# The last rounding pass of the FFN's weights: adding DMAs issued by GpSimd in place of a VectorE subtraction

## The chip, the cores and the metric

One core of a Trainium2 chip. The metric is the device time of one execution in microseconds, as the median over several runs. The engines are called by the profile's names: PE (TensorE), DVE (VectorE), ACT (ScalarE), POOL (GpSimd) and SP (SyncE, which here only issues DMAs).

## The reference

x is 2048 tokens by 512 features. The first layer normalizes x, projects it to q, k and v (16 heads of 32), and runs a chunked test-time-training scan: for each chunk of 16 tokens the state S of every head is read (k S and q S), a gradient-like v_new is made from it, and S is updated before the next chunk may read it. A gate, a norm and Wo follow, and the result is normalized and added to x. The second layer is a gated FFN (512 to 1536 to 512) with weights rounded to float8_e4m3:

```
wq = w.astype(jnp.float8_e4m3fn).astype(x.dtype)
gate = silu((x @ gate_wq) * gate_scale);  up = (x @ up_wq) * up_scale
y = ((gate * up) @ down_wq) * down_scale
```

So before the FFN can multiply, each of its 3 x 512 x 1536 weights has to be rounded to the values that float8_e4m3 has. The kernel does that itself, in float32 arithmetic.

## The kernel before

The 2048 tokens are 16 tiles of 128, and a tile is 8 chunks; "chunk 2.5" is chunk 5 of tile 2. All engines run the same timeline `body(t, s, h)` over the tiles, each its own list of instructions in a written order, tied by semaphores. In the body of tile t the scan of tile t runs; beside it the projections of tile t + 1 ("prep"), the tail of the attention of tile t - 1 ("post"), and the FFN of pairs of earlier tiles, cut into six rounds.

One chunk goes so. PE reads the state (`read_state`, L558 and L567). DVE's `scan_front` opens with a statistic (L1465) on it. POOL makes rho from that, a power of -1/2 (`scan_rho`, L1180), then rho2 and re. DVE's `scan_back` needs rho at L1487 and ends with VX (L1501). PE's `write_state` (L581, L589) multiplies VX, and DVE adds the product to the state (`scan_state`, SQ at L1508). PE may then read it for the next chunk. Work of the other stages is placed between these steps: on DVE between VX and the state sum, or behind the state sum and in front of the next L1465; on PE between the state read and the update, or behind the update. POOL's own roots of 16 columns (rk in chunk 3, rq in chunk 1, ro in chunk 5; 16 of each) are powers at L1180 too.

The rounding works on 36 units of 128 x 512 weights, one per chunk from chunk 0.0 to chunk 4.6 (none for chunk 2 of tiles 1 to 3; `unit_at`). A unit u takes these steps, all but the loads one chunk's length apart at most:
- SP loads it into buffer `wst[u % 2]`, which is a `yb` tile (`stage`, L357). The load of unit u + 2 waits until unit u is rounded (L396).
- DVE extracts a power of two from each weight's exponent into `wmg`, which is `x1[3]` (`exponent`, L1609), at the end of the chunk.
- ACT makes the "magic" number from it in two passes (`magic`, L998 and L1000), in the next chunk.
- `shift` subtracts: wst = wmg - wst. POOL does it behind VX (L1268) where `pool_free` holds; in chunk 3, and in chunks 1 and 5 from tile 1 on, DVE does (L1614): 26 and 10 units.
- DVE subtracts again and writes the weight matrix GW, UW or DW: w = wmg - wst (`quantize`, L1619).

The FFN's first products wait for their thirds of the weights (L637, L657). DVE's list of one chunk ends with shift (if it is DVE's), quantize and the exponent of the next unit; then comes the next chunk's `scan_front`.

PE's clock falls when it is little used. The prologue keeps it up with products that nobody reads (`idle`, L430: each call makes 2n products of 128 x 256, which are 4n PE instructions).

## Time and profile before

| | |
|---|---|
| median of 3 runs | 890.64 us (889.45 to 890.83) |
| the profiled execution | 887.37 us |
| its span (first to last instruction) | 885.6 us |
| PE busy | 793.8 us, 90% |
| DVE busy | 676.8 us, 76% |
| ACT busy | 496.7 us, 56% |
| POOL busy | 480.5 us, 54% |
| granted PE clock, mean | 0.953 |

A busy share is an average over the whole span. Which engine sets the pace differs between the stretch with the rounding (the first 284 us) and the rest, so the views by stretch and the waits matter more than this table. All times of the trace count from the span's start.

### The profile page before, as it was taken

The page shows a single profiled execution, that of the slowest core. Times are in us where ns is not written, and L with a number is a line of the kernel's source. Part 1 is how long each engine was busy: PE and PEld are TensorE (multiplying, and loading weights), DVE is VectorE, ACT ScalarE, POOL GpSimd, SP SyncE. Part 2 cuts the span into 40 slices and gives each one's busy share as a digit, 9 for nine tenths or more (in the row PEclk, how much of TensorE's full clock was granted, in tenths as well). Part 3 has the DMA queues.
Part 4 walks back from the last instruction along what each step waited for, and adds up shares of the span by engine and source line. Part 5 has one row for each costly group of instructions (what it writes and reads, how often), then busy time and mean ns, then how long its engine had stood idle before and what let it go on. Part 6 is the DMA issues. An engine that isn't in the chain of part 4 may idle for free.

```text
span 885.6 us, 22947 instructions
## 1 busy us (share of the span) xinstructions
PE 793.8 (90%) x8308; PEld 558.6 (63%) x8308; DVE 676.8 (76%) x2704; ACT 496.7 (56%) x1328; POOL 480.5 (54%) x848
## 2 busy tenths in 40 slices
PE   9867777688978999999999999999999999978896
PEld 4444444456566666667676676766676766766795
DVE  3688887788878787778787878778777878767444
ACT  2776675667657565655646475656565564633331
POOL 6355756565556656556465546565665646445300
PEclk9887798798989999999999999999999999979998
DMA  8012121211211001000100010000100010001000
GB/s 274 25 49 61 34 64 36 62 37 37 61 37 37 2 2 49 2 26 2 49 2 26 1 38 14 26 1 2 50 2 25 3 48 2 2 2 48 1 24 25
DMA packets 16721, 28.48 MB, mean 32 GB/s; under 512 B 3520, under 2 KB 3520, under 8 KB 16608
## 3 DMA queue, kind: packets, MB, share of 16 engines
q1 hardware_dynamic: 16608, 27.02, 9.9%
q8 instruction: 66, 1.08, 0.5%
q14 instruction: 47, 0.39, 0.1%
HBM read 22.82 MB, written 4.19 MB: 31 GB/s over the span
## 4 chain that ended last, share of the span: by engine, by line
PE 59%; DVE 17%; POOL 10%; ACT 7%; issue 6%; DMA 1%; SPq 1%; POOLq 0%; DVEq 0%; ACTq 0%
PE bank L630 17%; PE bank L426 15%; PE bank L663 8%; PE bank L606 4%; PE bank L581 4%; POOL rho L1180 3%; PE bank L440 3%; PE bank L558 2%; ACT BDk L893 2%; PE bank L567 2%; PE bank L589 2%; DVE work L1492 2%; DVE f L1574 1%; PE bank L454 1%; DVE work L1496 1%
## 5 line engine op out<-in xcount | busy, mean ns | idle before, releaser
L1180 POOL TENSOR_TENSOR rho<-sy,cst 128x2 f32<-128x2 f32 x128 | 89.5, 700 | 236.4 <-DVE sy L1465 236.4
L581 PEld LDWEIGHTS bank<-VX,BDkR 128*64 128x64 f32 x1024 | 45.1, 140 | 93.1 <-issue 53.1
L1508 DVE TENSOR_TENSOR SQ<-SQ,bank 128x128 f32<-128x128 f32 x128 | 36.6, 286 | 79.2 <-PE bank L581 78.0
L581 PE MATMUL bank<-VX,BDkR 128*64 128x64 f32 x1024 | 57.0, 233 | 40.4 <-DVE VX L1501 40.4
L948 ACT ACTIVATE qhR<-bank 128x64 f32<-128x64 f32 x128 | 28.2, 221 | 102.6 <-PE bank L589 102.0
L907 ACT ACTIVATE BDkR<-kR,cst 128x128 f32<-128x128 f32 x256 | 81.3, 397 | 0.0
L663 PE MATMUL bank<-DW,fh 128*128 128x512 f32 x188 | 80.4, 428 | 0.6 <-DVE fl L1581 0.6
L893 ACT ACTIVATE BDk<-bank 32x256 f32<-32x256 f32 x124 | 46.4, 374 | 53.8 <-DVE kR L1407 46.1
L663 PE MATMUL bank<-DW,fl 128*128 128x512 f32 x188 | 75.2, 400 | 0.0
L1487 DVE SCALAR_TENSOR_TENSOR work<-work,rho,rR 128x32 f32<-128x32 f32 x256 | 53.1, 248 | 25.9 <-POOL rho L1180 25.7
L558 PEld LDWEIGHTS bank<-SQ,BDk 128*64 128x64 f32 x1024 | 46.2, 142 | 38.5 <-issue 34.4
L567 PE MATMUL bank<-SQ,BDq 128*64 128x32 f32 x1024 | 54.8, 228 | 16.2 <-ACT qhR L948 15.0
L630 PE MATMUL bank<-xh,UW 128*128 128x256 f32 x384 | 66.2, 295 | 1.2 <-DVE f L1574 1.2
L630 PE MATMUL bank<-xh,GW 128*128 128x256 f32 x384 | 65.9, 294 | 1.4 <-DVE xl L1563 1.3
L558 PE MATMUL bank<-SQ,BDk 128*64 128x48 f32 x1024 | 57.2, 233 | 9.7 <-DVE SQ L1508 8.2
L426 PE MATMUL bank<-Wq,xnT 128*64 128x512 f32 x256 | 63.3, 633 | 0.7 <-ACT xnT L840 0.7
L606 PE MATMUL bank<-Wo,o 128*64 128x512 f32 x256 | 61.1, 621 | 1.7 <-DVE o L1545 1.7
L426 PE MATMUL bank<-Wv,xnT 128*64 128x512 f32 x256 | 62.5, 607 | 0.0
L630 PE MATMUL bank<-xl,GW 128*128 128x256 f32 x384 | 62.3, 285 | 0.0
L630 PE MATMUL bank<-xl,UW 128*128 128x256 f32 x384 | 61.6, 283 | 0.0
L426 PE MATMUL bank<-Wk,xnT 128*64 128x512 f32 x256 | 60.3, 611 | 0.0
L567 PEld LDWEIGHTS bank<-SQ,BDq 128*64 128x64 f32 x1024 | 44.8, 146 | 19.6 <-ACT qhR L948 11.6
(168 smaller groups left out, 2149.4 us busy)
## 6 DMA issues: line engine op xcount, KB each, us to landing
xt<-in_x SPq DMA_DIRECT2D x16, 256.0 KB, 2.8
x<-in_x SPq DMA_DIRECT2D x16, 256.0 KB, 2.8
out<-x SPq DMA_DIRECT2D x16, 256.0 KB, 2.1
yb<-in_gate_w SPq DMA_DIRECT2D x12, 256.0 KB, 2.7
yb<-in_up_w SPq DMA_DIRECT2D x12, 256.0 KB, 2.7
yb<-in_down_w SPq DMA_DIRECT2D x12, 256.0 KB, 2.7
Wk<-in_wk SPq DMA_DIRECT2D x1, 1024.0 KB, 6.1
Wv<-in_wv SPq DMA_DIRECT2D x1, 1024.0 KB, 7.9
```

Of the source, the lines that this page charges most:

```text
L426: ins = mm(dst[lo, :], half(xnT, k, lo), W[:, k * n:(k + 1) * n], start=(k == 0), stop=(k == KD - 1), skip_group_check=True)
L558: ins = mm(KAv[gp * 64:(gp + 1) * 64, gh, 0:48], bdk(s)[:, gh * NC + j, gp, :], SQv[:, 2 * gh + gp, :], start=True, stop=True, skip_group_ ...
L567: ins = mm(QH[gp * 64:(gp + 1) * 64, gh * DH:(gh + 1) * DH], bdq[:, j // 4, 2 * gp + gh, j % 4, :], S[:, 2 * gh + gp, :], start=(gh == 0), ...
L581: ins = mm(dS[p, e], bdkr[:, gh, j % 4, p], VX[:, e], start=True, stop=True, skip_group_check=True)
L606: ins = mm(PA[1][lo, :], half(ogT, g, lo), Wo[:, g * D:(g + 1) * D], start=(g == 0), stop=(g == 3), skip_group_check=True)
L630: ins = mm(b[:, q * PAIR:(q + 1) * PAIR], W[:, k * I + m * P:k * I + (m + 1) * P], part[:, k * PAIR:(k + 1) * PAIR], start=(part is xh and ...
L663: ins = mm(Y[k][:, :], part[:, q * PAIR + k * P:q * PAIR + (k + 1) * P], DW[:, m * D:(m + 1) * D], start=(m == 0 and n == 0), stop=(m == M ...
L893: ins = fn(bdk(s)[q, :, gp, own(h)], PA[1][p:p + 32, 256 * a:256 * a + 256].rearrange("p (m c) -> p m c", c=CH), ACT.Copy)
L907: ins = fn(bdkr[:, :, place, h * DH:(h + 1) * DH], kR[:, :].rearrange("p (gh j e) -> p gh j e", gh=2, e=DH)[:, :, js], ACT.Identity, scale ...
L1180: tt(dst, src, cst[:, C_NH:C_NH + n], ALU.pow).then_inc(*one)
L1487: stt(out=g2(g)[:, gh], in0=g2(u)[:, gh], scalar=rho[:, gh:gh + 1], in1=r_j[:, gh, :], op0=ALU.mult, op1=ALU.add).then_inc(*scan_v.one(f"g ...
L1508: tt(S, S, dS.rearrange("p (g e) -> p g e", e=DH), ALU.add).then_inc(*scan_v.one("S"))
```

## The change

The last subtraction goes from DVE to a DMA. ACT's second pass now writes the magic number straight into the unit's place in GW, UW or DW. POOL makes wst = wst - place for all 36 units, and then issues a DMA from wst onto the place that adds: place + (w - place). DVE keeps only the exponent. The semaphore for a rounded unit becomes two, one per buffer, counted in 16s, and those who wait for rounded weights wait for both. DVE's next exponent may start when ACT has read `wmg` (it waits for `s_magic`). In the chunks where `pool_free` doesn't hold, shift and DMA stand at the end of POOL's list of the chunk, behind its root. SP's load of unit u + 2 waits for the landing of unit u's adding DMA.

Two smaller parts come with it, both on PE. The gate product of tiles 2 and 3 moves from chunk 0 of its tile to chunk 6 of the tile before, behind the centring product. And unread products (`idle`) are put between state read and update: in tile 0 in chunks 4, 6 and 7 (12, 12 and 8 PE instructions), in tiles 1 and 2 in chunk 4 (12 each).

```diff
-        def quantized(third, n):
-            return s_quant, 12 * third + n
+        def quantized(n, k):
+            return s_quant[k], 16 * ((n + 1 - k) // 2)
+
+        def place(u):
+            w, e = unit(u)
+            return (GW, UW, DW)[w][:, e:e + D]
...
-                        sp.wait_ge(s_quant, UNITS)
+                        sp.wait_ge(s_magic, UNITS)
...
-                            sp.wait_ge(s_quant, u + 1)
+                            sp.wait_ge(s_quant[u % 2], 16 * (u // 2 + 1))
                             stage(u + 2)
...
             def prep_gate(t):
                 if early(t):
                     pe.wait_ge(*prep_a.at("g1", t))
+                    if t > 1:
+                        pe.wait_ge(*prep_a.at("th", t - 1))
...
             def ffn_g(p, r):
                 if p == 0:
-                    pe.wait_ge(*quantized(r // 2, 8))
+                    pe.wait_ge(*quantized(12 * (r // 2) + 8, 0))
+                    pe.wait_ge(*quantized(12 * (r // 2) + 8, 1))
...
-                        if early(t) and t > 1:
-                            prep_gate(t)
...
                     if j == 4 and early(t + 1):
                         prep_v_early(t + 1, (3,))
+                        pe.wait_ge(*(prep_v.at("kR", t) if t else prep_v.at("rR", 0)))
+                        idle(3, cst)
...
                         if early(t + 1):
                             prep_cen(t + 1)
+                            if t == 0:
+                                pe.wait_ge(*prep_v.at("kR", 1))
+                                idle(3, cst)
+                            else:
+                                prep_gate(t + 1)
...
                     if j == 7 and t == 0:
                         prep_gate(1)
+                        idle(2, cst)
...
-                fn(wmg[:, :], wmg[:, :], ACT.Identity, bias=epses[:, 6:7]).then_inc(s_magic, 1)
+                fn(place(u), wmg[:, :], ACT.Identity, bias=epses[:, 6:7]).then_inc(s_magic, 1)
...
             def shift(u):
                 pool.wait_ge(s_magic, u + 1)
-                tt(wst[u % 2][:, :], wmg[:, :], wst[u % 2][:, :], ALU.subtract).then_inc(s_shift, 1)
+                tt(wst[u % 2][:, :], wst[u % 2][:, :], place(u).bitcast(F32), ALU.subtract).then_inc(s_shift, 1)
+
+            def quantize(u):
+
+                pool.wait_ge(s_shift, u + 1)
+                nc.gpsimd.dma_start(place(u).bitcast(F32), wst[u % 2][:, :], accum_op=ALU.add).then_inc(s_quant[u % 2], 16)
...
                             shift(u)
+                            quantize(u)
...
+                    if scan and not pool_free(t, j):
+                        for u in unit_before(t, j):
+                            after_rows(NC * t + j)
+                            shift(u)
+                            quantize(u)
...
                 if u:
-                    dve.wait_ge(s_quant, u)
+                    dve.wait_ge(s_magic, u)
...
-            def shift(u):
-                dve.wait_ge(s_magic, u + 1)
-                tt(wst[u % 2][:, :], wmg[:, :], wst[u % 2][:, :], ALU.subtract).then_inc(s_shift, 1)
-
-            def quantize(u):
-                w, e = unit(u)
-                dve.wait_ge(s_shift, u + 1)
-                tt((GW, UW, DW)[w][:, e:e + D], wmg[:, :], wst[u % 2][:, :], ALU.subtract).then_inc(s_quant, 1)
...
-                    for u in unit_before(t, j):
-                        if not pool_free(t, j):
-                            shift(u)
-                        quantize(u)
```

## Rows read from the trace of the kernel before

**Rows 1.** Busy time by stretch, cut at tiles' starts: stretch and its length, PE, PEld, DVE, ACT, POOL busy, PE clock.

```profile
26.70:73.50 46.80, 33.12 (x392) 21.46 (x392) 36.09 (x152) 33.09 (x87) 23.38 (x39) 0.84 0.15 41
73.50:121.60 48.10, 37.49 (x396) 21.42 (x396) 40.02 (x159) 31.77 (x81) 28.49 (x42) 0.80 0.16 45
...
172.80:225.30 52.50, 44.03 (x466) 30.41 (x467) 43.26 (x169) 35.73 (x90) 31.70 (x51) 0.87 0.16 47
225.30:284.20 58.90, 50.02 (x514) 35.37 (x514) 47.25 (x178) 38.25 (x94) 33.58 (x52) 0.94 0.16 46
284.20:332.50 48.30, 46.68 (x518) 32.97 (x517) 39.64 (x165) 29.10 (x81) 28.84 (x55) 1.00 0.03 7
```

**Rows 2.** Line L1465 from 32 to 284 us: its instructions; idle time before them, times.

```profile
L1465 DVE BATCH_NORM_STATS2 sy<-bank x39: 221/228/236, 32.2 to 277.5; 128x6 f32<-128x68 f32 x39
...
  PE bank L558: 1.4, 1
```

**Rows 3.** Timeline of DVE, chunk 2.5: start, us, line, operation, count, [idle before it].

```profile
154.02 0.41 DVE L1487 SCALAR_TENSOR_TENSOR work<-work,rho,rR 128x32 f32<-128x32 f32 x2 [0.18 <-POOL rho L1180]
...
155.99 0.29 DVE L1508 TENSOR_TENSOR SQ<-SQ,bank 128x128 f32<-128x128 f32 x1
...
157.02 0.66 DVE L1614 TENSOR_TENSOR yb<-x,yb 128x512 f32<-128x512 f32 x1
157.72 0.69 DVE L1619 TENSOR_TENSOR UW<-x,yb 128x512 fp32r<-128x512 f32 x1
158.51 0.43 DVE L1609 TENSOR_SCALAR x<-yb 128x512 int32<-128x512 int32 x1
158.86 0.23 DVE L1465 BATCH_NORM_STATS2 sy<-bank 128x6 f32<-128x68 f32 x1
```

**Rows 4.** Timeline of PE, chunk 2.5: its read of the state.

```profile
156.43 0.44 PE L558 MATMUL bank<-SQ,BDk 128*64 128x48 f32 x8 [0.27 <-DVE SQ L1508]
```

**Rows 5.** Groups of instructions, whole span: count, busy us, mean ns, idle before.

```profile
L1268 POOL TENSOR_TENSOR yb<-x,yb 128x512 f32<-128x512 f32 x26 | 35.1, 1350 | 33.3 <-DVE VX L1501 23.8 <-ACT x L1000 9.5
...
L1619 DVE TENSOR_TENSOR DW<-x,yb 128x512 fp32r<-128x512 f32 x12 | 9.3, 771 | 0.4 <-POOL yb L1268 0.2
...
L1619 DVE TENSOR_TENSOR GW<-x,yb 128x512 fp32r<-128x512 f32 x12 | 9.1, 760 | 0.1
...
L1619 DVE TENSOR_TENSOR UW<-x,yb 128x512 fp32r<-128x512 f32 x12 | 8.4, 704 | 0.1
...
L1614 DVE TENSOR_TENSOR yb<-x,yb 128x512 f32<-128x512 f32 x10 | 6.7, 665 | 0.0
```

**Rows 6.** Timeline of POOL, chunk 2.5: its root of 16 columns.

```profile
154.58 2.90 POOL L1180 TENSOR_TENSOR ro<-oss,cst 128x16 f32<-128x16 f32 x1
```

**Rows 7.** Timeline of DVE, chunk 1.3.

```profile
93.83 0.41 DVE L1487 SCALAR_TENSOR_TENSOR work<-work,rho,rR 128x32 f32<-128x32 f32 x2 [0.99 <-POOL rho L1180]
```

**Rows 8.** Timeline of SP: one issue of a load of 256 KB.

```profile
29.79 0.33 SPq L385 DMA_DIRECT2D xt<-in_x  x1
```

**Rows 9.** DMA issues: count, KB each, median us from issue to landing.

```profile
out<-x SPq DMA_DIRECT2D x16, 256.0 KB, 2.1
yb<-in_gate_w SPq DMA_DIRECT2D x12, 256.0 KB, 2.7
```

**Rows 10.** Busy time by stretch, as rows 1, of chunk 1.0.

```profile
73.50:80.00 6.50, 5.71 (x44) 2.57 (x44) 4.21 (x20) 3.90 (x9) 2.34 (x4) 0.58 0.25 81
```

**Rows 11.** Timeline of DVE, chunk 1.0: its state sum.

```profile
78.66 0.29 DVE L1508 TENSOR_TENSOR SQ<-SQ,bank 128x128 f32<-128x128 f32 x1 [1.12 <-PE bank L581]
```

**Rows 12.** Timeline of PE: prologue, chunk 0.6 and chunk 1.0.

```profile
7.91 1.08 PE L434 MATMUL bank<-work 128*64 128x256 f32 x8
...
64.57 0.45 PE L581 MATMUL bank<-VX,BDkR 128*64 128x64 f32 x8 [2.07 <-DVE VX L1501]
...
74.50 3.68 PE L426 MATMUL bank<-Wq,xnT 128*64 128x512 f32 x8 [0.69 <-ACT xnT L840]
```

**Rows 13.** Waits from 20 to 284 us: who for whom, us in all, times, longest.

```profile
DVE work L1487 <- POOL rho L1180: 8.8, 40, 1.0
```

More of the change, by code:

```diff
@@ L181, in build @@
         s_stage = [sem(f"s_stage{n}") for n in range(len(wst))]
-        s_exp, s_over, s_magic, s_shift, s_quant = (sem(n) for n in ("s_exp", "s_over", "s_magic", "s_shift", "s_quant"))
+        s_exp, s_over, s_magic, s_shift = (sem(n) for n in ("s_exp", "s_over", "s_magic", "s_shift"))
+        s_quant = [sem(f"s_quant{n}") for n in range(2)]
         s_mask = sem("s_mask")
@@ L656, in ffn_down @@
                     if p == 0:
-                        pe.wait_ge(*quantized(r // 2, 12))
+                        pe.wait_ge(*quantized(12 * (r // 2) + 12, 0))
+                        pe.wait_ge(*quantized(12 * (r // 2) + 12, 1))
                     if r == 0 and p > 0:
@@ L1587, in fin_y @@
                 else:
-                    dve.wait_ge(s_quant, UNITS)
+                    dve.wait_ge(*quantized(UNITS, k))
                 if p == 0 and k == 0:
```

## The prediction

> **What bounds the kernel now.** I read the windows cut at the starts of tiles 0 to 5 first. Tile 5, the first with no weights to round, takes 48.3 us, and the PE is busy for 46.7 of it at full clock. Tiles 0 to 3 take 46.8 to 52.5 us, but their PE is busy for only 33 to 44 us and its granted clock is 0.80 to 0.87 (tile 4 is 58.9 us at 0.94) [rows 1]. So up to about 284 us something other than the PE sets the pace, and all the rounding lies there. Next the line that opens each chunk, the VectorE's L1465: in chunks 0.1 to 4.7 (tile.chunk, 39 of them) it waited for the PE once, for 1.4 us in all [rows 2]. It is otherwise behind other VectorE work.
>
> The timeline of chunk 2.5 shows which. The VectorE has written VX by 155.44, the PE answers with the update, and the state sum SQ runs from 155.99 to 156.28. Then come a statistic of the next x, the shift (0.66), the rounding subtraction L1619 (0.69) and the exponent (0.43), until the next chunk opens at 158.86 [rows 3]. The PE's read of the state started at 156.43 and ended at 156.87 [rows 4]: the answer lay there 2 us before it was read. From SQ's end the PE needs 0.59 us in such a chunk. The rest is what a lighter VectorE can win, until the PE's answer or another resource is late.
>
> **What the change takes off the VectorE.** 36 subtractions L1619 are 9.3 + 9.1 + 8.4 us and 10 shifts L1614 are 6.7 us: 33.5 us, all of it in front of an L1465 that doesn't wait for the PE [rows 5]. The state sum of these chunks is not delayed by it. Where the PE has products of its own in front of the state read, the gain stops at its end: chunk for chunk that costs 1.6 us of the 33.5.
>
> **What it puts on POOL.** The 26 shifts that POOL has stay (1.35 us of its time each, 1.27 undisturbed), the 10 others come to it, and 36 DMAs are issued there [rows 5]. POOL also computes rho, on which the VectorE waits in every chunk, so anything that is still running on POOL 0.31 us after a chunk opens delays the chunk. There are two sorts of chunk.
> - Where POOL has a root of 16 columns (2.90 us, chunk 2.5 as the example: from 154.58 to 157.48 [rows 6]; chunks 1 and 5 of a tile, and 3), the shift and DMA go behind it. The old next opening was 158.86; less shift and subtraction it would be 157.5. POOL would end at 157.48 + 1.27 + 0.1 + the issue. With an issue of 1.0 us that is 159.85, and rho, wanted at 157.8, is 2 us late where 1.35 was won. Ten units are of this sort.
> - Elsewhere the shift starts just after VX, is done 3.9 us after the opening, and with the DMA POOL is free at 5.0: in time where nothing follows (chunks 0, 5, 7), late by up to 3 us where POOL's own list goes on. In chunk 1.2 it goes on so far that rho of 1.3 was late by 0.8 us already (L1487 waited 0.99 us for it, against the usual 0.18 [rows 3, 7]). The issue is added to that whole, and the VectorE gets there 1.75 us sooner: 3.4 us late.
>
> **The issue is not in the trace.** From below: SP spends 0.33 us on issuing 256 KB [rows 8]. From above: a POOL instruction over a whole tile, 1.35 us [rows 5], and somewhat beyond, since an adding DMA has two tiles to address: 1.5 us. Nothing makes it a gain. I take 1.0 us, nearest to the POOL rows since POOL does the work, and 0.3 and 1.5 for the range.
>
> **The landing isn't either.** Plain DMAs of 256 KB land 2.1 us (store) and 2.7 us (load of weights) after their issue [rows 9]. The adding one reads twice. I take 2.6 us after POOL has issued, from 2.1 to 4. It matters since SP loads unit u+2 into the buffer of unit u only after the landing, and the VectorE's exponent of u+2, which stands in order in front of the next chunk's opening, waits for that load. The loop of one buffer is: exponent 0.43, opening to VX 2.55, shift until 3.9, wait and issue until 5.0, landing 7.6, load 10.4, exponent. It may take two chunks, 10.6 to 12 us. So it just fits in the light chunks, and is 1 to 2 us late behind a chunk with a root. What queues behind the waiting exponent is the whole chain: the next chunk's statistics, rho, VX, the state.
>
> **The sum.** I carried these rules through chunks 0.0 to 5.7 in order, with each chunk's own VectorE work, PE times and POOL list; on the old placement they give the start of tile 6 within 0.3 us of the trace's. For the change: 33.5 us off, 1.6 back at the PE's end, 22.6 back where rho is later, 10.4 back in exponents that wait for their load, and 5.1 off again, since in chunks where the PE was late anyway (it ends its own products after VX) a late VX costs less. Together -4.0 us. The two unseen prices decide: 0.3 and 2.1 give -16.0; 1.0 and 2.1 give -5.9; 1.3 and 2.6 give +2.1; 1.5 and 3.0 give +9.8; 1.0 and 4.0 give +7.8.
>
> **The gate and the unread products.** The gate of tiles 2 and 3 moves from chunk 0 to chunk 6 of the tile before. In chunk 0 it ran in front of the VectorE's VX; in chunk 6 it runs there too, behind a centring that in chunk 0.6 left the PE idle for the last 2.07 us before the update [rows 12]: 16 PE instructions of 128 columns, about 1.1 us at full clock, fit. Nothing, either way, with 0.5 us each at half clock if they don't. The products are 56 PE instructions at 0.135 us (1.08 us for 8 [rows 12]), 7.6 us in all, at most 12 at a time (1.6 us) between the state read and the update, where the PE idled about 2 us [rows 12]: nothing at full clock, though 3.2 us each at half clock, which would hold the update by up to 1 us in five chunks. What they can bring is clock. Chunk 1.0 ran at 0.58 [rows 10]: 8 instructions on Wq took 3.68 us [rows 12], which at full clock would be half, and the state sum waited 1.12 us for the update behind them [rows 11]. If they hold, that wait goes, plus 0.1 to 0.2 us in some ten chunks whose update ran slow. I take -1.5 us, from -3 to +4. SP's x loads, and the FFN's waits for units 8, 20, 32 and 12, 24, 36, come over a microsecond after the landings: nothing.
>
> **Two rules of the Trainium skill.** The shift and exponent rows show a VectorE instruction with one input over 512 elements at 0.43 us where one with two takes 0.66 or more [rows 3, 5]. The Trainium skill's page "SBUF — State Buffer", section "SBUF: two separate sides", says that a GpSimd-issued DMA's descriptors can't be written while the VectorE runs in its two-port mode; the exponent falls about where POOL would issue. No run here shows it. By that rule half of the issues would take 0.43 us more, and my sum would lose some 4 us: it would be about zero. The page "DMA: Bandwidth & Descriptors", section "Anatomy of one DMA — SWDGE (gpsimd) path", puts a whole DMA of this kind at 2.0 us plus bytes / 436 GB/s, an estimate of 2.6 us for 256 KB where I took 3.6 for issue and landing, though it is a figure for plain copies; by it the sum would be 3 us better.
>
> **The rivals.**
> - POOL is cheap: the issue costs what SP's does, the landing is a store's. -16 - 2: 872.6 us. For it: SP's row. Against: POOL's rows are two to four times those of the VectorE for the same tile.
> - The loop of load, rounding, adding and loading is too long (slower). It decides from the point where issue and landing together pass 3.2 us in light chunks: each exponent then waits, up to 29 us in the sum at 1.0 and 4.0, and the time is 890.6 + 7.8 = 898.4 us; with a dear issue (1.5, 3.0) rho carries it instead: 900.4. For it: the load must follow the landing, and ten units are late already. Against: nothing in the trace takes 4 us for 256 KB with the queues empty.
> - The relief and POOL's lateness cancel (1.2 and 2.6, or the lock above): within 1.8 us of 890.6.
>
> **How the numbers follow.** The profiled execution was 887.4 us, 1.8 around a span of 885.6; the median is 890.64, and I take the difference off that: -4.0 - 1.5 = -5.5, 885.1 us. Chances: forecast (876 to 888.8) 0.38, cheap POOL (below 876) 0.19, cancel 0.13, slower rival 0.30. Within 0.2% (1.8 us, about what can be told from no change) is 0.13. The range from 873 to 900 leaves out the ends.
>
> **What would show it.** Right: tiles 0 to 4 together shorter by 4 to 7 us, tiles from 5 on unchanged; L1487 waiting for rho over 1 us in chunks 2, 4, 6 and those behind a root, some 20 us over the 8.8 of now [rows 13]; about 10 us of waits in front of L1609 for loads. Wrong: rho waits as now (issue below 0.3), or L1609 waiting in nearly every chunk (landing near 4), or L581 behind unread products.

## The result and the profile after

The changed kernel takes 907.53 us (median of 4 runs, 905.43 to 908.25) against 890.1 us before (4 runs, 889.45 to 890.83). The ratio is 1.0194, with a 95% interval of 1.018 to 1.0208: slower by 17.4 us. The forecast was 885.1 us, faster by 5.5, in a range from 873 to 900. Size and sign were wrong. The profiled execution of the changed kernel took 905.43 us, its span is 903.6 us and its mean granted clock 0.952.

The lines of the kernel have moved: L1465 is now L1493, L1487 L1515, L1475 L1503, L1609 L1637, L1268 L1285, L1508 L1536, L1400 L1428, and the new DMA is L1290. L1268 is now POOL's product qR over a whole tile (L1251 before).

First the windows cut at the starts of tiles 0 to 5, as [rows 1] (stretch and length; PE, PEld, DVE, ACT, POOL busy; clock; DMA). Tile 2 of before, which [rows 1] leaves out, then all of after:

```profile
121.60:172.80 51.20, 36.55 (x404) 20.80 (x400) 42.21 (x169) 32.12 (x81) 31.00 (x50) 0.87 0.16 48
```

```profile
30.30:78.70 48.40, 36.69 (x422) 23.70 (x423) 33.02 (x144) 33.24 (x87) 31.30 (x47) 0.83 0.33 72
78.70:128.60 49.90, 35.97 (x412) 21.32 (x410) 37.23 (x151) 31.20 (x80) 37.54 (x51) 0.89 0.37 80
128.60:184.00 55.40, 38.71 (x411) 21.95 (x408) 38.63 (x160) 32.52 (x82) 40.24 (x60) 0.85 0.35 77
184.00:241.50 57.50, 44.02 (x459) 29.84 (x459) 39.69 (x161) 35.99 (x90) 40.94 (x60) 0.82 0.33 74
241.50:301.10 59.60, 50.65 (x523) 35.75 (x521) 40.73 (x167) 38.06 (x94) 44.86 (x63) 0.94 0.35 77
301.10:350.60 49.50, 47.63 (x522) 33.69 (x521) 39.71 (x166) 29.02 (x81) 28.77 (x55) 1.00 0.07 17
```

Tiles 0 to 4 are longer by 1.6, 1.8, 4.2, 5.0 and 0.7 us, 13.3 in all, tile 5 by 1.2. The DVE's busy time in tiles 0 to 4 fell by 3.1, 2.8, 3.6, 3.6 and 6.5 us, 19.5 together, where 33.5 us of instructions were taken off it. POOL's rose by 8 to 11 us a tile. The first chunk also opens later, at 30.3 instead of 26.7 us. Most of that is scatter between executions: it opens at 27.3 to 28.6 us in the three experiments without GpSimd's DMAs and at 27.0 to 31.0 in the nine with them, and SP's issue of Wg in front of it took 1.67 us in the trace of before, 4.23 here, and from 1.67 to 4.29 in the traces of the experiments, with and without those DMAs. That a microsecond of it belongs to the change is not excluded. So single traces are compared by their tiles below, not by their spans.

The second view is the page's chain that ended last, by engine; of before, then of after.

```profile
PE 59%; DVE 17%; POOL 10%; ACT 7%; issue 6%; DMA 1%; SPq 1%; POOLq 0%; DVEq 0%; ACTq 0%
```

```profile
PE 52%; POOL 18%; DVE 12%; issue 6%; ACT 5%; DMA 5%; SPq 0%; POOLq 0%; ACTq 0%; DVEq 0%
```

The DVE's share of the path fell by 5 points, as meant. POOL's rose by 8 and the DMAs' by 4. The groups say at which prices (line, engine, operation, count, busy us, mean ns, idle before). First a row of before that is not among those ahead of the prediction, then after:

```profile
L1475 DVE SCALAR_TENSOR_TENSOR work<-mP,work 128x64 f32<-128x64 f32 x128 | 27.5, 215 | 0.0
```

```profile
L1503 DVE SCALAR_TENSOR_TENSOR work<-mP,work 128x64 f32<-128x64 f32 x128 | 33.2, 259 | 0.0
L1637 DVE TENSOR_SCALAR x<-yb 128x512 int32<-128x512 int32 x36 | 22.2, 617 | 6.5 <-DMA yb<-in_gate_w 3.2 <-DMA yb<-in_down_w 2.3 <-DMA yb<-in_up_w 1.0
...
L1290 POOL DMA_DIRECT2D GW<-yb x12 | 11.2, 932 | 3.6 <-POOL yb L1285 3.6
L1290 POOL DMA_DIRECT2D UW<-yb x12 | 11.1, 922 | 3.6 <-POOL yb L1285 3.6
L1290 POOL DMA_DIRECT2D DW<-yb x12 | 11.0, 916 | 3.6 <-POOL yb L1285 3.6
```

And from the DMA issues, as [rows 9] (KB, median us from issue to landing):

```profile
UW<-yb POOLq DMA_DIRECT2D x12, 256.0 KB, 3.4
```

An issue costs POOL 0.92 us and 0.30 us of idle time between the end of the shift and the DMA (3.6 us for 12), 1.22 us together, 36 times: 44.1 us. The landing comes 3.4 us after the start of the issue, 2.4 to 2.5 after its end. And two instructions of the DVE have become longer without having changed: the exponent from 0.425 us [before, 15.3 us for 36] to 0.617, and L1503 from 0.215 to 0.259: 6.9 and 5.7 us.

The third view is the DVE's waits in tiles 0 to 4 (who for whom: us in all, times, longest). Before, beside the row for rho in [rows 13]:

```profile
DVE SQ L1508 <- PE bank L581: 17.3, 18, 2.9
...
DVE kss L1391 <- ACT xn_dv_rT L871: 4.9, 2, 2.6
DVE bx L1400 <- POOL bt L1208: 3.8, 4, 1.9
```

After:

```profile
DVE work L1515 <- POOL rho L1197: 26.1, 39, 2.0
DVE SQ L1536 <- PE bank L590: 15.9, 15, 2.9
DVE bx L1428 <- POOL bt L1225: 9.2, 5, 2.9
DVE kss L1419 <- ACT xn_dv_rT L888: 7.7, 2, 4.6
...
DVE x L1582 <- ACT x L981: 3.5, 1, 3.5
DVE x L1637 <- DMA yb<-in_gate_w: 3.2, 4, 1.3
DVE x L1637 <- DMA yb<-in_down_w: 2.3, 3, 1.5
...
DVE x L1637 <- DMA yb<-in_up_w: 1.0, 2, 0.8
```

The wait for rho is 17.3 us longer. The other names belong to the preparation of the next tile (bt, kss) and to the tail of an earlier one (nb_f, x). bt, another output of POOL, is waited for by 5.4 us more, and kss by 2.8, over ACT, which in its turn waited for POOL's nb_f for 13.2 us in these tiles instead of 8.2 (7.36 us of it in chunk 2.2, where the DVE then waited 4.64 us for kss). The loads take 6.5.

One place shows how the new list of POOL works on both engines. In chunk 2.4 POOL goes from the shift to the DMA to qR; then the DVE's exponent of the same chunk (start, us, line, operation, [idle before]):

```profile
160.57 1.27 POOL L1285 TENSOR_TENSOR yb<-yb,UW 128x512 f32<-128x512 f32 x1 [1.19 <-DVE VX L1529]
162.14 0.94 POOL L1290 DMA_DIRECT2D UW<-yb  x1 [0.30 <-POOL yb L1285]
162.80 1.59 POOL L1268 TENSOR_TENSOR qR<-qR,bR 128x512 f32<-128x512 f32 x1
```

```profile
162.65 2.02 DVE L1637 TENSOR_SCALAR x<-yb 128x512 int32<-128x512 int32 x1
```

The exponent starts at 162.65, while POOL issues, and ends at 164.67, 0.28 us after qR did, for 0.43 us of work. It is not the issue alone that does this. In chunk 0.2 an exponent lies wholly inside an issue, with no whole-tile POOL instruction beside it, and keeps its length (POOL, then DVE):

```profile
47.01 0.91 POOL L1290 DMA_DIRECT2D GW<-yb  x1 [0.31 <-POOL yb L1285]
```

```profile
47.21 0.42 DVE L1637 TENSOR_SCALAR x<-yb 128x512 int32<-128x512 int32 x1
```

Of the 36 exponents 8 took over 0.5 us, and 7 of these ran beside a whole-tile POOL instruction, a shift or qR; with an issue alone beside them six took 0.41 to 0.43 us and one 0.57. What makes the three of 2.0 to 2.5 us is the pair: they start during an issue, before qR's record starts, and end 0.3 us behind qR. L1503 is the same: its 8 instances over 0.5 us all overlap a shift or POOL's whole-tile product L1275, and the longest, 1.79 us in chunk 1.3, starts in an issue.

And behind the root of chunk 2.5, the case that the prediction took as its example, in chunk 2.6:

```profile
169.16 1.43 POOL L1285 TENSOR_TENSOR yb<-yb,UW 128x512 f32<-128x512 f32 x1
170.90 0.94 POOL L1290 DMA_DIRECT2D UW<-yb  x1 [0.30 <-POOL yb L1285]
171.56 1.03 POOL L1197 TENSOR_TENSOR rho<-sy,cst 128x2 f32<-128x2 f32 x1
```

```profile
172.69 0.41 DVE L1515 SCALAR_TENSOR_TENSOR work<-work,rho,rR 128x32 f32<-128x32 f32 x2 [2.01 <-POOL rho L1197]
...
177.33 0.36 DVE L1428 TENSOR_TENSOR bx<-bt,cst 128x64 f32<-128x64 f32 x2 [1.69 <-POOL bt L1225]
```

The DVE waits 2.01 us for rho, of which 0.18 is usual: some 1.8 us late, where 2 was worked out. The same lateness then runs on in POOL's list: VX is late, the next shift and DMA with it, bt stands behind that DMA, and the DVE waits another 1.69 us in the same chunk. That second wait was not in the sum.

### The profile page after: what moved, and what is told of

Its sections match the earlier page's. It is cut to its first block, busy times and chain, and to the rows that moved or that the text cites. A ratio compares the mean times of both kernels' runs of the same rounds, so it can differ in the third digit from the quotient of the medians.

```text
span 903.6 us, 23071 instructions
## 1 busy us (share of the span) xinstructions
PE 799.1 (88%) x8364; PEld 561.8 (62%) x8364; DVE 657.5 (73%) x2658; ACT 496.9 (55%) x1328; POOL 527.4 (58%) x894
## 4 chain that ended last, share of the span: by engine, by line
PE 52%; POOL 18%; DVE 12%; issue 6%; ACT 5%; DMA 5%; SPq 0%; POOLq 0%; ACTq 0%; DVEq 0%
PE bank L639 16%; PE bank L433 14%; PE bank L674 7%; POOL rho L1197 4%; POOL yb L1285 4%; PE bank L590 3%; PE bank L615 3%; PE bank L447 3%; PE bank L567 2%; POOL rq L1197 2%; PE bank L576 2%; POOL ro L1197 2%; ACT BDk L910 2%; DVE work L1520 1%; PE bank L598 1%
## 5 line engine op out<-in xcount | busy, mean ns | idle before, releaser
L1197 POOL TENSOR_TENSOR rho<-sy,cst 128x2 f32<-128x2 f32 x128 | 93.4, 730 | 194.1 <-DVE sy L1493 193.9
L1536 DVE TENSOR_TENSOR SQ<-SQ,bank 128x128 f32<-128x128 f32 x128 | 36.6, 286 | 77.7 <-PE bank L590 76.5
L1515 DVE SCALAR_TENSOR_TENSOR work<-work,rho,rR 128x32 f32<-128x32 f32 x256 | 53.1, 248 | 43.8 <-POOL rho L1197 43.1
```

The lines of the kernel that those rows point to most:

```text
L1197: tt(dst, src, cst[:, C_NH:C_NH + n], ALU.pow).then_inc(*one)
L1515: stt(out=g2(g)[:, gh], in0=g2(u)[:, gh], scalar=rho[:, gh:gh + 1], in1=r_j[:, gh, :], op0=ALU.mult, op1=ALU.add).then_inc(*scan_v.one(f"g ...
L1536: tt(S, S, dS.rearrange("p (g e) -> p g e", e=DH), ALU.add).then_inc(*scan_v.one("S"))
```

## The experiments

Three theories were to be told apart. Theory 1: POOL's time for the issues, which delays rho and what stands behind it in POOL's list. Theory 2: the DVE's instructions are slowed while POOL issues. Theory 3: the loop of load, add and next load is too long. All runs are compared with the kernel before on the same chip (medians 889.8 to 890.0 us).

**The two halves of the change.** `small_alone` is the kernel before with this alone:

```diff
 def prep_gate(t):
                     pe.wait_ge(*prep_a.at("g1", t))
+                    if t > 1:
+                        pe.wait_ge(*prep_a.at("th", t - 1))
...
-                        if early(t) and t > 1:
-                            prep_gate(t)
...
+                        pe.wait_ge(*(prep_v.at("kR", t) if t else prep_v.at("rR", 0)))
+                        idle(3, cst)
...
+                            if t == 0:
+                                pe.wait_ge(*prep_v.at("kR", 1))
+                                idle(3, cst)
+                            else:
+                                prep_gate(t + 1)
...
+                        idle(2, cst)
```

> The kernel before with the gate of tiles 2 and 3 behind the centring and with the unread products; the rounding stays as it was. Theory (the whole loss is the adding DMAs'): my -1.5 us stands, within -3 to +1 of the kernel before, 887 to 891 us, and the prologue ends where it did, first chunk at 26.7 us. Rival (the unread products and the gate hold up the update): 3 to 4 us slower, with the state sum L1508 waiting for L581 more than before in tiles 0 to 2.

889.27 us, ratio 0.9991 (0.9977 to 1.0006). `dma_alone` is the changed kernel with these lines taken back:

> The changed kernel with the gate where it was and without the unread products. Theory (the loss is the adding DMAs'): the ratio of the changed kernel within 3 us, 906 to 911 us. Rival (the small parts are what costs): under 895.

909.16 us, ratio 1.0215 (1.0188 to 1.0242). So the loss is the rounding's alone, and the small parts bring 1 to 2 us or nothing. They do not do what I took them for: in chunk 1.0 of `small_alone` the update still came late behind products on Wq at the lower clock (timelines of PE and DVE). In the changed kernel these 8 instructions took 1.94 us instead of 3.68, but in `dma_alone`, without the unread products, they took 1.94 as well:

```profile
76.15 3.68 PE L426 MATMUL bank<-Wq,xnT 128*64 128x512 f32 x8 [0.69 <-ACT xnT L848]
```

```profile
80.31 0.29 DVE L1516 TENSOR_TENSOR SQ<-SQ,bank 128x128 f32<-128x128 f32 x1 [1.12 <-PE bank L583]
```

**The relief without its price.** `no_adds` is the changed kernel with the DMA taken out. A unit counts as done when POOL has shifted it; the last addition of the rounding is thus left out.

```diff
-                tt(wst[u % 2][:, :], wst[u % 2][:, :], place(u).bitcast(F32), ALU.subtract).then_inc(s_shift, 1)
+                tt(wst[u % 2][:, :], wst[u % 2][:, :], place(u).bitcast(F32), ALU.subtract).then_inc(s_quant[u % 2], 1)
...
-                nc.gpsimd.dma_start(place(u).bitcast(F32), wst[u % 2][:, :], accum_op=ALU.add).then_inc(s_quant[u % 2], 16)
+                pass
```

> The changed kernel with its 36 adding DMAs left out (so the weights stay the magic numbers, not the rounded weights); all 36 shifts stay on POOL and a buffer is free as soon as the shift is done. Theory that the loss is what the issuing of the DMA costs (POOL's time, some 1.2 us each with the gap, and the VectorE instructions that run longer beside it) and its landing: all of the 33.5 us off the VectorE shows except what the PE and the 10 late shifts give back, some 865 to 875 us; the exponent is back at about 0.43 us mean. Rival that the 10 shifts behind the roots are the cost: 885 to 895. If POOL's shift and not its DMA makes the exponent long, the mean of the exponent stays near 0.6 us.

872.46 us, ratio 0.9804 (0.979 to 0.9819): 17.6 us faster than before. The exponent is short again, and the wait for rho is up from 9 to 17 us, where POOL's list has only the shifts behind the roots more than before (group, and wait over 27 to 290 us):

```profile
L1636 DVE TENSOR_SCALAR x<-yb 128x512 int32<-128x512 int32 x36 | 15.7, 436 | 0.0
```

```profile
DVE work L1514 <- POOL rho L1197: 17.4, 43, 1.9
```

The adding DMAs therefore cost 907.5 - 872.5 = 35.1 us, twice what the rest of the change brings.

**The DMA put on top of the kernel before.** `issue_only` leaves the rounding as it was and issues 35 adding DMAs in vain:

```diff
+            def add_nothing(u):
+                if u == 0:
+                    pool.wait_ge(s_wq, 16)
+                    pool.wait_ge(s_void, 1)
+                else:
+                    pool.wait_ge(s_add, 16 * u)
+                if u < UNITS - 1:
+                    nc.gpsimd.dma_start(DW[:, 11 * D:12 * D].bitcast(F32), Wq[:, 0:D], accum_op=ALU.add).then_inc(s_add, 16)
```

> The kernel before (subtractions and all on the VectorE as they were) with 35 adding DMAs of 256 KB issued by POOL at the places of the change, onto a place that is not yet written, and for which only the last subtraction waits. Theory 1 (POOL's time for the issue delays rho and its other outputs): +10 to +20 us, waits of L1487 for rho up from 9 to some 20 us. Theory 2 (the VectorE's instructions run longer beside the issue): mean of the exponent and of the two-input instructions up by the same 0.1 to 0.2 us as in the changed kernel, some 10 us of the loss. Theory 3 (the loop of load, add and load costs): under 2 us, since nobody waits for the landing. Prologue: if a GpSimd DMA in the program is what delays Wk's landing and the first chunk (26.7 to 30.3 us), it does here too; if not, 26.7.

903.23 us, ratio 1.0147 (1.0128 to 1.0167): 13.2 us, so theory 3 can't be the main cause. The waits for rho rose to 10.8 us only, less than theory 1 had, since here the DVE still has its subtractions and gets to rho later; those for bt and kss rose as well, from 3.8 to 5.2 and from 4.9 to 6.4 (over 27 to 290 us). Of the DVE I was half right. The exponent stayed at 0.426 us, the five that started during an issue included, but now the subtractions are long (0.70 to 0.77 us before [rows 5]):

```profile
L1637 DVE TENSOR_TENSOR GW<-x,yb 128x512 fp32r<-128x512 f32 x12 | 10.8, 899 | 0.1
L1637 DVE TENSOR_TENSOR DW<-x,yb 128x512 fp32r<-128x512 f32 x12 | 10.3, 858 | 0.4 <-POOL yb L1269 0.3
```

Seven of them took over 0.8 us, and all seven ran beside a whole-tile POOL instruction; one of the seven started in an issue. The kernel before has four such, without any DMA of POOL: one subtraction took 1.75 us beside POOL's product over o. So the issue lengthens DVE instructions mostly by moving POOL's whole-tile instructions beside others of the DVE.

**The same in the lighter schedule.** `no_adds_issue` puts such DMAs into `no_adds`, where no buffer waits for them:

```diff
-                pass
+                if u == 0:
+                    pool.wait_ge(s_wq, 16)
+                    pool.wait_ge(s_void, 1)
+                else:
+                    pool.wait_ge(s_add, 16 * u)
+                pool.wait_ge(s_quant[u % 2], u // 2 + 1)
+                if u < UNITS - 1:
+                    nc.gpsimd.dma_start(DW[:, 11 * D:12 * D].bitcast(F32), Wq[:, 0:D], accum_op=ALU.add).then_inc(s_add, 16)
```

> The kernel without the adds (its weights stay the magic numbers; 872.5 us), with 35 adding DMAs put back on POOL at the places of the change, but from Wq onto a place not yet written, so that no buffer waits for their landing. Theory 1 and 2 (what costs is the issue: POOL's time, and the VectorE beside it): 893 to 903 us, at least two thirds of the 35 us between no_adds and the changed kernel, with the exponent long again (0.55 to 0.65 us mean) and rho waited for by some 25 us. Theory 3 (the loop through landing and load): below 883 us.

912.25 us, ratio 1.0253 (1.0225 to 1.028), above the range and 5 us above the changed kernel. The edit had a cost of its own: POOL stood 6.6 us waiting for the landing of the DMA before. `no_adds_issue2` takes that away:

```diff
-                    pool.wait_ge(s_add, 16 * u)
+                    pool.wait_ge(s_add[u % 2], 16 * (u // 2))
...
-                    nc.gpsimd.dma_start(DW[:, 11 * D:12 * D].bitcast(F32), Wq[:, 0:D], accum_op=ALU.add).then_inc(s_add, 16)
+                    v = UNITS - 1 - u % 2
+                    nc.gpsimd.dma_start(place(v).bitcast(F32), Wq[:, 0:D], accum_op=ALU.add).then_inc(s_add[u % 2], 16)
```

> As no_adds_issue, but the 34 adding DMAs go in turn onto two places not yet written, so that none waits for the landing of the one before it (in no_adds_issue that was 6.6 us of POOL's time). It leaves out the same part, the adding of the units. If the 912 us came from the issue itself: 903 to 909 us, the same as the changed kernel. If from that wait: under 897.

908.36 us, ratio 1.0213 (1.0185 to 1.0241): the whole loss, with no load waiting for a landing. It is not quite clean either, since POOL idled 0.53 us in front of each DMA instead of 0.30.

**POOL's time against its ports.** `no_adds_pow` has in place of each DMA an instruction that holds POOL as long and moves five columns:

```diff
-                pass
+                pool.wait_ge(s_quant[u % 2], u // 2 + 1)
+                tt(pw[:, :], cst[:, C_ONE:C_ONE + 5], cst[:, C_NH:C_NH + 5], ALU.pow)
```

> The kernel without the adds, with a power of 5 columns on POOL in place of each adding DMA (some 1.2 us of POOL's time: the DMA's 0.92 and the 0.30 of idle in front of it), which hardly touches the memory. Theory 1 (POOL's time alone is the cost): within 4 us of no_adds_issue2. Theory 2 (the VectorE is slowed by POOL's port use around the issue): the exponent back at 0.44 us mean, and 8 to 14 us faster than no_adds_issue2.

899.62 us, ratio 1.011 (1.0096 to 1.0125). Groups, and the wait over 27 to 290 us:

```profile
L1291 POOL TENSOR_TENSOR pw<-cst 128x5 f32<-128x5 f32 x36 | 43.2, 1201 | 2.8
```

```profile
L1638 DVE TENSOR_SCALAR x<-yb 128x512 int32<-128x512 int32 x36 | 17.3, 480 | 0.0
```

```profile
DVE work L1516 <- POOL rho L1198: 28.7, 38, 3.4
```

46.0 us on POOL (43.2 + 2.8) against the DMAs' 44.1, and 27.2 us of the time come with it: 21 us for each microsecond of POOL time per unit (27.2 / 1.28), though nothing here is a DMA. In tiles 0 to 4 its trace is 26.9 us longer than that of `no_adds`, and there the DVE waits 12.8 us more for rho (29.4 for 16.6), 6.8 more for bt, 2.4 more for kss and 2.9 more for the PE at the state sum. The kernel is 7.9 us faster than the changed one and 8.7 faster than `no_adds_issue2`. By the expectation's own words that is theory 2's range and not theory 1's; the dummies held POOL 3.5 us less than those DMAs did (46.0 for 31.6 + 17.9), which at 27.2 / 46.0 is 2 of the 8.7. The exponent came near its old length, not back to it, and the long ones show that no DMA is needed for it (POOL, then DVE, chunk 1.4):

```profile
106.24 1.27 POOL L1269 TENSOR_TENSOR qR<-qR,bR 128x512 f32<-128x512 f32 x1
```

```profile
106.75 1.04 DVE L1638 TENSOR_SCALAR x<-yb 128x512 int32<-128x512 int32 x1
```

**The loop.** `buf3` is the changed kernel with a third buffer:

```diff
+        def buf(u):
+            return u % 3 if u < 27 else (u - 27) % 2
+        def room(u):
+            return (yb[0], yb[1], x1[2])[buf(u)][:, :]
```

> The changed kernel with three buffers for the loads of weights up to unit 26 (the third is x1[2], which nobody uses before tile 4), two after that. Theory 3 (the loop): the 6.5 us of exponents that wait for loads go nearly all, and with them 6 to 10 us of the time, 898 to 902 us. Theory 1 and 2: the VectorE gets to the next rho sooner and waits there instead, 903 to 908 us.

904.81 us, ratio 1.0167 (1.015 to 1.0184): no exponent waits any more, and the median is 2.7 us lower. That is what theories 1 and 2 gave and less than theory 3 did. Even the 2.7 is not clear of noise: the interval overlaps that of the changed kernel (from 1.018), and in its trace tiles 0 to 4 take 272.3 us against 270.8. The long exponents stayed (9 of them):

```profile
L1650 DVE TENSOR_SCALAR x<-x 128x512 int32<-128x512 int32 x9 | 6.1, 682 | 0.0
```

**The issue in another place.** `deferred3` is `buf3` with the DMA of a unit one chunk later, right behind re, where POOL waits for VX in any case:

```diff
                         scan_rho(t, j, s)
+                        for u in unit_before(t, j - 1):
+                            quantize(u)
...
                             shift(u)
-                            quantize(u)
```

> As buf3, and the adding DMA of a unit is issued one chunk later, right behind re, where POOL waits for VX anyway. Theory 1 (what costs is that the issue stands behind the shift and in front of the next rho): near the kernel without the adds, 872 to 882 us, the wait for rho back at some 17 us. Theory 2 (the VectorE is slowed wherever POOL issues): the VectorE's two passes in front of VX, on the chain of every chunk, run 0.2 to 0.4 us longer, 36 times, and it is 884 to 892 us.

897.28 us, ratio 1.0083 (1.0056 to 1.0109). 7.5 us better than `buf3`, but 15 us above the range of theory 1 and 5 above that of theory 2; the mean of L1516 (the old L1475), at 0.232 us, had come down, so it was not theory 2 that was missing. The loop had come back: exponents waited 8.7 us for loads. `deferred3_dve` gives the 10 shifts behind the roots back to the DVE:

> As deferred3, with the 10 shifts of the chunks with roots back on the VectorE (0.67 us each). If POOL's lateness behind roots costs more than the 6.7 us: 3 to 6 us faster than deferred3; if less: up to 5 us slower.

888.84 us, ratio 0.9994 (0.9981 to 1.0008): 8.4 us better, more than forecast, though it puts 6.7 us back on the DVE. So behind a root the shift on POOL cost 8.4 + 6.7 = 15.1 us for 10 units, 1.5 us each, if all of the DVE's 0.67 us is on the path there; the two intervals leave some 3 us of doubt in the 8.4. The timeline of POOL in chunk 2.7 of `deferred3_dve` shows the new place of the DMA; rho2 and re end at 161.16, the shift waits for VX still 0.34 us:

```profile
161.09 0.92 POOL L1303 DMA_DIRECT2D UW<-yb  x1
162.35 1.27 POOL L1298 TENSOR_TENSOR x<-x,DW 128x512 f32<-128x512 f32 x1 [0.34 <-DVE VX L1538]
```

The mean of L1512 (the old L1475) was 0.218 us here and that of the exponent 0.445 to 0.449: next to nothing of theory 2 is left. Exponents still waited 9.1 us for loads. What else kept the gain small is new. SP's list (issues):

```profile
170.09 0.33 SPq L373 DMA_DIRECT2D x<-in_down_w  x1
170.46 0.43 SPq L401 DMA_DIRECT2D xt<-in_x  x1
170.94 0.43 SPq L410 DMA_DIRECT2D x<-in_x  x1
```

```profile
ACT x L994 <- DMA x<-in_x: 9.9, 2, 6.2
```

SP issues the two loads of x in its list for tile 3, one of them the residual for the tail, only after it has waited for the last unit of tile 2, whose DMA now comes a chunk later. The tail's ACT waits 9.9 us in all for such loads. `deferred3_sp` moves SP's own wait a chunk later too:

```diff
-                    for u in unit_before(t, j):
+                    for u in unit_before(t, j - 1):
                         for v in then(u):
```

> deferred3_dve with SP's load of the next weights moved one chunk later in SP's list as well, so that its load of a tile's x for the residual no longer stands behind a wait for the tile's last unit. Theory (in deferred3_dve the VectorE waited 9.0 us in front of x L1591 because of that load): 4 to 8 us faster than its 888.8, 881 to 885 us. Rival (the tail has slack elsewhere): within 2 us of it.

885.04 us, ratio 0.9939 (0.9917 to 0.9961), at the edge of the range; the wait is gone, and the exponents' wait for loads is 11.9 us. `best` finishes the last nine units, which have two buffers only, by an addition on the DVE; SP's waits for these units go back to where they were:

```diff
+                        if u >= 27:
+                            dve.wait_ge(s_shift, u + 1)
+                            tt(place(u), place(u).bitcast(F32), room(u), ALU.add).then_inc(s_fin, 1)
```

> deferred3_sp with units 27 to 35, which have two buffers only, finished by an addition on the VectorE (0.7 us each, 6.3 us) in place of the DMA. Theory (those units' exponents wait 9.1 us for loads behind a landing one chunk late): 2 to 4 us faster than deferred3_sp, 878 to 883 us, and faster than the kernel before. Rival: the VectorE's additions cost what the waits did, within 2 us of deferred3_sp.

879.73 us (5 runs), ratio 0.9884 (0.9867 to 0.9902): it beats both kernels, and `deferred3_sp` by 5.3 us, more than forecast. Its windows of tiles 0, 1 and 3, and its wait for rho in tiles 0 to 4:

```profile
30.24:74.30 44.06, 34.98 (x422) 21.76 (x423) 30.81 (x145) 32.89 (x87) 28.39 (x45) 0.87 0.34 73
74.30:119.00 44.70, 35.68 (x410) 20.41 (x409) 34.74 (x153) 31.10 (x80) 34.66 (x49) 0.90 0.40 89
...
166.50:216.50 50.00, 40.85 (x462) 27.03 (x463) 39.18 (x163) 35.74 (x90) 38.05 (x58) 0.93 0.38 85
```

```profile
DVE work L1530 <- POOL rho L1215: 14.8, 40, 1.9
```

## Where the 17.4 us come from

| from | to | us |
|---|---|---|
| before (890.0) | no_adds (872.5) | -17.6: the DVE relieved, all shifts on POOL, the small parts |
| no_adds | no_adds_pow (899.6) | +27.2: POOL held 1.2 us longer per unit |
| no_adds_pow | buf3 (904.8) | +5.2: that it is a DMA |
| buf3 | after (907.5) | +2.7, not clear of noise: exponents that wait for loads |

Each step has an uncertainty of some 2 us. The steps come from different kernels and need not add in another order. The third compares a power that held POOL for 46.0 us with DMAs that held it for about 44, so the DMA's own share is rather 6 than 5. It goes with 4.9 us more of DVE busy time in tiles 0 to 4 (189.2 for 184.2), nearly all of it in three DVE instructions that start in an issue with a whole-tile POOL instruction behind it. The other long DVE instructions are in `no_adds` and `no_adds_pow` too. Why such a start is held until POOL's next instruction ends is not shown: no run took the DMA's port use away alone.

One thing moves with the second step and is not separated from it. The granted clock of tiles 0 to 4 was 0.87 to 0.97 in `no_adds` and 0.84 to 0.92 in `no_adds_pow`, and the PE was busy for 203.9 us there instead of 195.4. On the DVE's side 2.9 us of this show, in the waits of the state sum.

## The prediction, point by point

The terms of the sum beside the traces of tiles 0 to 4, before and after (us; busy times and waits overlap a little and need not add up to the last one):

| term | forecast | trace |
|---|---|---|
| DVE relieved | -33.5 | -19.5 (busy) |
| back where the PE's read ends last (waits in front of the opening statistic) | +1.6 | +1.6 |
| waits for rho | +22.6 | +17.3 |
| exponents that wait for loads | +10.4 | +6.5 |
| absorbed by the PE's own lateness (state sum) | -5.1 | -1.4 |
| waits for bt and kss | none | +8.2 |
| the tail's x, behind ACT and a load | none | +2.3 |
| together | -4.0 | +15.0; the tiles are 13.3 longer |

- **The steps that failed**: three terms of the sum. The relief was taken at its full 33.5 us on the ground that the instructions left on the DVE keep their lengths; 14.0 of it did not come. POOL's outputs other than rho stood at nothing, and cost 8.2. And slack was to absorb 5.1 us of lateness, and took 1.4. Rho and the loads, which the sum did have, came out below it.
- **What bounds the kernel**: right. With the subtractions off the DVE and nothing in their place the kernel gains 17.6 us (`no_adds`). That this is close to the rival in which POOL is cheap (issue 0.3, landing 2.1: -16 - 2, 872.6 us) is partly luck: the rival still has an issue and a landing, `no_adds` has neither.
- **The prices of issue and landing**: nearly right. I took 1.0 and 0.1 us, and 2.6 to the landing; 0.92 and 0.30, and 2.4 to 2.5 were measured, so 0.12 us more on POOL. The sum had -4.0 at 1.0 and +2.1 at 1.3, so the measured price makes about 2.4 us of difference, and with the small parts some 887 to 888 us. The other 20 us of the miss are not a price. They are the step from POOL's time to the kernel's, the terms above.
- **rho**: 22.6 us forecast, 17.3 in the trace, some 1.8 us late in the example where 2 was worked out. The longest wait for rho anywhere was 2.0 us; 3.4 had been worked out for chunk 1.3, where the trace has 1.86. There the DVE itself got to rho later, behind the L1503 of 1.79 us. But the sum had only rho and the chain behind it. POOL's other outputs, which stand behind the DMA in its list, came late as well: bt by 5.4 us, kss over ACT by 2.8.
- **The 5.1 us that the PE's own lateness should absorb**: the state sum's wait for the PE fell from 17.3 to 15.9 us only, and in `dma_alone` it rose (20.0 against 18.3 us from 27 to 290 us).
- **A microsecond on POOL**: the sum had 14 us for it at the cheap end (from -16.0 at 0.3 and 2.1 to -5.9 at 1.0 and 2.1) and 20 at the dear end (from 1.0 to 1.3 at 2.6); the dummies measured 21 from nothing on. So it was the first microsecond that the sum had too cheap.
- **The DVE's own instructions**: they grew by 6.9 (exponent) and 5.7 us (L1503), 12.6 of the 14.0 us that the relief lacked. 4.7 of the 5.7 are there in `no_adds` already (0.251 us mean for L1502): seven of its eight instances over 0.5 us run beside a shift that stands behind a root and so meets the opening of the next chunk.
- **The rule of the shared ports**: I weighed the Trainium skill's page "SBUF — State Buffer", section "SBUF: two separate sides", in one direction: the VectorE would hold up GpSimd's descriptors, 4 us. The DMA's mean stayed at 0.92 us and was nowhere near 0.43 longer. The other direction of the same section of the Trainium skill holds: it calls the shared pair of ports an exclusive lock, kept for a whole instruction by whoever starts first, and the trace agrees, with an exponent of 1.04 us in `no_adds_pow` that starts during qR and ends 0.28 us behind it. The one of 2.02 us in the changed kernel ends 0.28 us behind qR too, but starts before qR's record, inside the issue. By the Trainium skill's page "DMA: Bandwidth & Descriptors", section "Anatomy of one DMA — SWDGE (gpsimd) path", the estimate for a DMA was 2.6 us; the adding ones took 3.4.
- **The loop**: 10.4 us forecast for exponents that wait for loads, 6.5 in the trace, at most some 3 of the time. As the slower rival (898.4 at a landing of 4) it was wrong: the landing was short. Its other form, a dear issue (1.5 and 3.0, 900.4), was nearest, but by a price that was not measured, and the mechanism it named (rho) was only part. Both numbers leave out the -1.5 of the small parts, which the forecast has.
- **SP's x loads "over a microsecond after the landings: nothing"**: in the changed kernel ACT waited once, for 3.4 us, for such a load (x L981, behind it the DVE's 3.5). In `deferred3_dve` it was 9.9 us. Wrong, and it cost most where the DMA was moved.
- **The small parts**: -1.5 forecast, -0.8 measured alone (-2.0 to +0.5) and -1.6 on top of the DMAs (907.5 for 909.2). The size fits, though no run tells it from nothing; the reason was not right: chunk 1.0's wait of 1.12 us stayed when they were alone and went without them in `dma_alone`.
- **What would show it**: waits over 1 us behind roots and in the chunks after long POOL lists, right; tiles 5 on unchanged, right but for 1.2 us of tile 5, which `no_adds` has too (49.5 us); tiles 0 to 4 shorter, wrong. None of the three signs that I had named for being wrong appeared: rho was waited for, 9 exponents of 36 waited for a load, and the updates did not stand behind unread products. The signs covered the terms of the sum and not what it left out.

## What to carry to other kernels

Work moved to an engine with a low busy share (POOL had 54%) is not free if each output of that engine is awaited in order: follow everything behind the new work in its list, not only the next output. An instruction of that kind belongs where the engine waits for something in any case, and every other queue that waits in order for its result has to be moved with it (here SP's), or the gain goes there. Nor is the relieved engine relieved by all that is taken off it: here 14 of 33.5 us did not come, since instructions left on it now met the other engine's. The sum that carried one chain and let slack absorb lateness erred on the good side; price a microsecond on the new engine by a dummy instruction in its place before trusting it.

## What the runs showed of the hardware

- An adding DMA of 256 KB within the on-chip memory, issued by GpSimd, holds POOL for 0.92 us, after 0.30 us of idle time where it waited for POOL's own last result (0.53 in `no_adds_issue2`). It had none in `issue_only` and `deferred3`, where it waited for nothing recent. It lands 2.4 to 2.5 us after its issue has ended in the changed kernel, 3.4 after its start; in `issue_only`, reading another tile, 3.7 after its start.
- A DVE instruction that started beside a whole-tile POOL instruction could end only behind it: 1.04 us for 0.43 (exponent, `no_adds_pow`), 1.75 for 0.77 (the mean of such a subtraction, before). One that started during an issue with such a POOL instruction behind it did so too: 2.02 us for 0.43 (exponent) and 1.79 for 0.215 (L1503, only 64 columns) in the changed kernel. Beside an issue alone DVE instructions kept their lengths, whole-tile ones too but for one exponent of 0.57 us: 0.42 us in chunk 0.2, and the five exponents that started during issues in `issue_only` at 0.43. In `deferred3_dve` the DMA stands beside the instructions in front of VX, of 32 to 128 columns; they kept theirs (0.25, 0.24 and 0.29 us in chunk 2.7, as in the changed kernel).
